# Packing two columns' bits into one f16 weight, and two last blocks of 68 rows

## The reference, cut to what is computed

```python
N, F, C = 5000, 128, 16                      # adj is 5000 x 5000 float32 of zeros and ones
# layer 0
w = adj * (y @ y.T)                          # y: one class of 16 for each row
w = w / maximum(w.abs().sum(1), 1e-12)
x = layernorm(x + 0.9 * (w @ x) + 0.1 * h0)
# layer 1, with adj for both of its matrices
f = tanh(adj * adj) * (adj > 0)              # tanh(1) where adj is one
new_adj = the 350 largest of each row of f   # a row has fewer than 350 ones
h2 = tanh(x @ W_proj + b_proj)
x = layernorm(x + relu(new_adj @ (h2 @ W_gcn) + b_gcn))
```

## Time and profile before

| | us |
|---|---|
| median of 3 runs | 467.92 (467.48 to 468.11) |
| the profiled execution | 467.66 |
| its span, first to last instruction | 465.9 |
| PE busy | 438.7 (94%) |
| DVE busy | 377.9 (81%) |
| ACT busy | 263.5 (57%) |
| POOL busy | 161.5 (35%) |
| adj's DMAs | about 3 to 259 |

### The profile page before, as it was taken

The page is one execution under the profiler, slowest core; times in us unless marked ns, Lnnn a source line. Parts: engine busy times, 40 slices in busy tenths (PEclk is TensorE's granted clock), DMA queues, the critical chain, the costliest instruction groups (busy, mean ns, idle before and its releaser), DMA issues.

```text
span 465.9 us, 15131 instructions
## 1 busy us (share of the span) xinstructions
PE 438.7 (94%) x5104; PEld 386.3 (83%) x5104; DVE 377.9 (81%) x1359; ACT 263.5 (57%) x355; POOL 161.5 (35%) x310
## 2 busy tenths in 40 slices
PE   3659999999999999999999999999999999999994
PEld 2448898888888988888888887888888888888883
DVE  5988999999999999999999976675575575575562
ACT  4997998999999999999999934900000000000000
POOL 3022543455444455554445541221211211211222
PEclk9977999999999999999999999999999999999998
DMA  8999999999999999999999200000000000000000
GB/s 262 411 414 420 419 417 417 415 408 411 409 422 420 422 423 420 424 423 412 417 419 422 60 2 1 13 11 17 17 11 17 17 11 17 17 11 17 17 11 23
DMA packets 25518, 108.50 MB, mean 233 GB/s; under 512 B 5097, under 2 KB 15490, under 8 KB 15490
## 3 DMA queue, kind: packets, MB, share of 16 engines
q1 hardware_dynamic: 25490, 108.14, 57.5%
HBM read 105.57 MB, written 2.56 MB: 232 GB/s over the span
## 4 chain that ended last, share of the span: by engine, by line
PE 75%; DVE 10%; ACT 5%; issue 5%; DMA 2%; POOL 2%; POOLq 0%; DVEq 0%; ACTq 0%; SPq 0%
PE acc L521 64%; PE words L471 6%; DVE a_bits L783 3%; DMA a_rows<-in_adj_dram 2%; PE feat_acc L584 2%; PE proj_acc L595 2%; ACT count_out L685 2%; DVE turned L870 2%; PE xnt_acc L576 1%; ACT count_out L678 1%; ACT x_parts L664 1%; POOL xs L438 1%; ACT count_out L754 1%; DVE z_high L921 1%; ACT count_out L746 1%
## 5 line engine op out<-in xcount | busy, mean ns | idle before, releaser
L521 PE MATMUL acc<-x_parts,turned 128*128 128x257 f16 (+1 forms) x1600 | 195.2, 276 | 3.2 <-DVE turned L870 1.0
L678 ACT ACTIVATE count_out<-a_rows,ones 128x2688 bf16<-128x2688 f32 (+1 forms) x80 | 190.2, 2377 | 0.5 <-DMA a_rows<-in_adj_dram 0.2
L521 PEld LDWEIGHTS acc<-x_parts,turned 128*128 128x128 fp8e4 (+1 forms) x1600 | 154.4, 98 | 28.9 <-issue 3.8
L521 PE MATMUL acc<-f_parts,turned 128*128 128x256 f16 (+1 forms) x1560 | 171.6, 273 | 0.8 <-DVE turned L870 0.8
L521 PEld LDWEIGHTS acc<-f_parts,turned 128*128 128x128 fp8e4 (+1 forms) x1560 | 152.0, 98 | 19.3 <-issue 1.3
L783 DVE TENSOR_SCALAR a_bits<-a_rows 128x2688 bf16<-128x2688 f32 (+1 forms) x80 | 116.7, 1459 | 2.7 <-DMA a_rows<-in_adj_dram 2.3
L421 POOL TENSOR_TENSOR var_eps<-mean_var,consts 128x1 f32<-128x1 f32 x80 | 18.6, 232 | 266.1 <-DVE mean_var L1077 139.7
L870 DVE TENSOR_SCALAR turned<-a_words 128x320 uint16 (+1 forms) x305 | 66.9, 233 | 53.2 <-PE acc L521 52.8
L424 POOL TENSOR_TENSOR rstd<-var_eps,consts 128x1 f32<-128x1 f32 x80 | 86.5, 1081 | 6.3
L870 DVE TENSOR_SCALAR turned<-same_class 128x320 uint16<-128x320 uint16 x313 | 71.3, 254 | 0.1
L471 PEld LDWEIGHTS words<-pack,a_bits 128*128 128x128 bf16 (+1 forms) x1600 | 51.3, 97 | 9.7 <-DVE a_bits L783 7.8
(11 more groups left out here) (111 smaller groups left out, 288.3 us busy)
## 6 DMA issues: line engine op xcount, KB each, us to landing
a_rows<-in_adj_dram SPq DMA_DIRECT2D x39, 1344.0 KB, 7.8
a_rows<-in_adj_dram SPq DMA_DIRECT2D x39, 1156.0 KB, 8.3
out_dram<-xn SPq DMA_DIRECT2D x39, 64.0 KB, 1.5
h_rows<-in_L_gnn_h_dram SPq DMA_DIRECT2D x19, 128.0 KB, 8.1
xs<-in_x_dram SPq DMA_DIRECT2D x3, 640.0 KB, 10.0
xs<-in_x_dram SPq DMA_DIRECT2D x1, 512.0 KB, 10.3
y_nat<-in_L_gnn_y_dram SPq DMA_DIRECT2D x1, 304.0 KB, 3.6
a_rows<-in_adj_dram SPq DMA_DIRECT2D x1, 84.0 KB
```

Source lines behind the costliest of these rows:

```text
L521: mm = pe.matmul(acc[par][0:m, 0:cols], bits, parts[:, b, 0:cols], start=first and b == blocks[0], stop=last and b == blocks[-1])
L678: act.activation(count_out[0:m, 0:w], a_rows[par][h][0:m, 0:w], ACT.Relu, bias=ones[0:m, 0:1], scale=-HUGE, accum_out=col).then_inc(s_coun ...
```

## The change

Rows and columns: there are now 38 full blocks, all in pairs, and the last 136 rows are two blocks of 68 (even and odd rows of them), so that still 40 blocks stand. Halves are 2560 and 2440 columns wide (20 column blocks each, 40 in all).

Packing: DVE writes a bit as a byte, 0x3C or 0x3D, into a uint8 tile. Two neighbouring bytes, which belong to the two blocks of a pair of columns, are read as one f16 weight. A packing matmul then takes 128 such weights (256 columns of adj), with `pack` as 128 x 17 f16; there are 10 a half, 20 a block. A word holds 8 rows of two columns; the count too is of two columns. ACT subtracts in `words_of` what the 0x3C bytes add up to, by a bias, with Relu and a scale; for the blocks of 68 rows in three pieces. Unpacking is eight shifts of 320 words a block as before (five for a block of 68 rows), but the fp8 bits of a column block now lie at every other byte, and the products read them so. In the setup, the packing weights need nine small steps on POOL in place of sixteen and three on DVE, the classes' words are made by half as many and as wide products, and the separate loads of block 0 of x, y and h0 are gone. SP loads h0 for a pair in odd steps, in place of even ones.

```diff
-BITS = 16
+BITS = 8
-    FULL = N // P
-    TAIL = N - FULL * P
-    NB = FULL + 1
+    FULL = N // (2 * P) * 2
+    TAIL = (N - FULL * P) // 2
+    NB = FULL + 2
+    COLS = NB // 2
     WORDS = P // BITS
-    HB = NB // 2 + 1
+    HB = NB // 2
+    HC = COLS // 2
...
     def rows_of(t):
-        return TAIL if isinstance(t, int) and t == LAST else P
+        return TAIL if isinstance(t, int) and FULL <= t <= LAST else P
...
     def rows_in(a, b, par, pair, cols):
-        if isinstance(b, int) and b == LAST:
-            return a[FULL * P:N, cols]
...
+        if isinstance(b, int) and b >= FULL:
+            return a[FULL * P:N, cols].rearrange("(p e) c -> e p c", e=2)[par]
+        v = a[0:FULL * P, cols].rearrange("(s p e) c -> e s p c", p=P, e=2)[par]
...
-        a_bits = [sb(f"a_bits{h}", [P, HB * P], BF16) for h in range(2)]
+        a_bits = [sb(f"a_bits{h}", [P, HB * P], U8) for h in range(2)]
...
-                for b in range(h * HB, HB if h == 0 else NB):
-                    c, d = column(b) - HALF[h].start, spacing(b)
+                for b in range(h * HC, h * HC + HC):
+                    c = (b - h * HC) * P
                     mm = pe.matmul(words[par][:, b * PITCH:b * PITCH + WORDS + 1],
-                                   a_bits[h][0:m, c:c + (P - 1) * d + 1:d], pack[0:m, :], start=True, stop=True)
+                                   a_bits[h][0:m, :].bitcast(F16)[:, c:c + P], pack[0:m, :], start=True, stop=True)
...
-                    bits = turned_at(n, par)[:, b, :].bitcast(F8)[:, 0:m]
+                    bits = turned_at(n, par)[:, b // 2, :].bitcast(F8)[:, b % 2:2 * m:2]
...
+                    if rows_of(n) == P:
+                        act.activation(to[:, :, 0:WORDS + 1], of[:, :, 0:WORDS + 1], ACT.Relu, bias=less_full, scale=UNIT)\
+                            .then_inc(s_words, 1)
+                        return
...
-                dve.tensor_scalar(a_bits[h][0:m, 0:w], a_rows[par][h][0:m, 0:w], 1.0, None,
-                                  ALU.is_equal).then_inc(s_bits, 1)
+                dve.tensor_scalar(a_bits[h][0:m, 0:w], a_rows[par][h][0:m, 0:w], 1.0, float(ZERO_BYTE),
+                                  ALU.is_equal, ALU.add).then_inc(s_bits, 1)
```

More of the change, by code:

```diff
@@ L77, in rows_in, with steps @@
     def rows_in(a, b, par, pair, cols):
-        if isinstance(b, int) and b == LAST:
-            return a[FULL * P:N, cols]
-        if isinstance(b, int) and b == 0:
-            return a[0:P, cols]
-        v = a[P:FULL * P, cols].rearrange("(s p e) c -> e s p c", p=P, e=2)[(par + 1) % 2]
-        if isinstance(b, int):
[L85 to L99, removed]
+        if isinstance(b, int) and b >= FULL:
+            return a[FULL * P:N, cols].rearrange("(p e) c -> e p c", e=2)[par]
+        v = a[0:FULL * P, cols].rearrange("(s p e) c -> e s p c", p=P, e=2)[par]
+        if isinstance(b, int):
+            return v[pair]
+        return v[bass.ds(pair, 1), :, :].rearrange("a p c -> p (a c)")
+    def steps(eng, step, lag, after={}, first=4):
+        first = max(first, lag + 2 + lag % 2)
         for t in range(first):
@@ L103, in steps @@
                 after[t]()
-        with eng.Fori((first - 1) // 2, (FULL - 1) // 2) as i:
+        with eng.Fori(first // 2, FULL // 2) as i:
+            step(i * 2, 0, i)
             step(i * 2 + 1, 1, i)
-            step(i * 2 + 2, 0, i + 1)
         for t in range(FULL, NB + lag):
@@ L121, in steps4 @@
             step(t, t % 2, t // 2, 0, t)
-        count = (FULL - first) // 4
-        with eng.Fori(0, count) as i:
+        with eng.Fori(0, (FULL - first) // 4) as i:
             for c in range(first, first + 4):
                 step(i * 4 + c, c % 2, i * 2 + c // 2, i, c)
-        for t in range(first + count * 4, NB + lag):
+        assert (FULL - first) % 4 == 0 and first % 2 == 0
+        for t in range(FULL, NB + lag):
             step(t, t % 2, t // 2, 0, t)
@@ L369, in step @@
                     load_rows(t, par, pair)
[L370 to L372 removed]
+                if valid(t - 1) and c >= 3 and par == 1:
+                    load_h0(t - 1, pair, i, c - 1)
+            steps4(sp, step, 4, 6)
             def store(t, par, pair):
@@ L388, in _ @@
                                base=0, pattern=[[-1, P]], channel_multiplier=1).then_inc(s_const, 1)
[L389 to L393, removed]
-                                       compare_op=ALU.not_equal, fill=float(1 << (bit + half * HALF_BITS)),
-                                       base=-(bit * 2 * WORDS + half), pattern=[[-2, WORDS]],
-                                       channel_multiplier=1).then_inc(s_pack, 1)
+            pool.wait_ge(s_pack, 2)
@@ L865, in unpack @@
                     dve.wait_ge(s_acc, n - 1)
-                last = HALF_BITS if m == P else 1
-                for bit in range(lo // 2, min(hi // 2, last)):
+                last = -(-m // WORDS)
+                for bit in range(lo, min(hi, last)):
                     shift = ONE_BIT - bit
```

253 lines of the change are left out of this document (134 added, 119 removed).

## The result

The changed kernel takes 489.65 us, median of its four runs, against 467.86 us for the kernel before on the same chip. One of the four took 2372 us; the other three have a median of 488.72 us (485.33 to 490.59), and by them the kernel takes 1.0436 times as long, with a 95% interval of 1.0365 to 1.0507. Forecast were 478.6 us (467 to 487) and slower: the direction is right, the time is past the upper end. The same kernel in a second set of runs took 485.41 us (483.08 to 486.02), 1.0364 times 467.83 (1.0332 to 1.0395). In all later runs of the kernel and of its variants nothing like it recurred; its cause is open, and so is whether the general path ran in it.

The account below looks back on a forecast made before the run. PE, DVE and the loads were taken as full at once, the loads' ceiling limiting gains; 467.66 + 8.0 (holding the steady -1.0) + 2.4 clock + 0.3 store = 478.4, with the runs' median 0.26 higher: 478.6 us, range 467 to 487.

Parts of the forecast that it names:

- An engine has moved 417.5 / 16 = 26.1 GB/s, four move 104, and 2.72 MB take 26.0 us: Last two blocks: four loads of 68 rows go to four engines; last packing +8.0 us, range 6.5 to 26.0 for the loads.
- The forecast's 15% on this rate: Last loads: uncertainty of the four engines' rate, 4 us to each side, used for the range 467 to 487.
- The steady part: Full blocks of layer 0: loads at their ceiling let PE's saving give only -1.0 us, 0 to 3 over 38 blocks.
- Cast, ten packings and hand-over: After the last half lands at 276.0: 1.35, 0.25 and 0.15 us, so the last packing ends at 277.8.
- The clock: After the last packing: PE's granted clock, lowered by the waits, slows products (+2.1) and packings (+0.3); +2.4 us, bounds 0 to 3.
- The end: Last store of 68 rows, 35 KB on four engines at 26.1 GB/s: +0.3 us.
- The number of engines: Loads of 68 rows: the most engines up to 16 that divide 68 are 4, DMA share near 0.25.
- the four waits in the last loads: Last loads: PE waits for DVE's cast, and that for a_rows, four times 3 to 5 us.
- casts at 1462 ns: DVE's cast to bytes: 0 added, near 1.46 us as before; bounds 0 to +1.45 us a half.
- the weights at every other byte: PE's products: byte-wise steps cost 0, loads near 97 ns; bounds 0 to tens of ns a product.
- packings at 24 ns: PE's packing matmuls: 24.3 ns each despite 17 columns, 20 a block, giving PE back 0.49 us a block.
- The rival of 16 engines: Last loads: all 16 engines serve 68 rows, 1.5 to 6 us gained, about 464; chance 0.12 for sixteen or eight engines.

Follow-up runs that it names:

- the split one: The changed kernel with each load of 68 rows in the two last blocks issued as one of 64 and one of 4 rows: 468.61 us, ratio 1.0003.

## Why the prediction was wrong in size and right in direction

**The step that failed: "An engine has moved 417.5 / 16 = 26.1 GB/s, four move 104, and 2.72 MB take 26.0 us".** Count, share and bytes were right, the rate wasn't. From 250 us on the trace moves 3.66 MB by 290.6, of which 2.72 are the last four loads; the other 0.94 need 2.2 us at 417.5, so the full loads end near 252.2 and the four take 38.4 us: 71 GB/s, 18 an engine. This term is +12.4 us. The second profiled execution, whose last packing ended 3.6 us earlier, comes to about 35 us and 77 GB/s in the same way. An engine's rate was taken from 16 engines with eight rows each. By themselves, loads of 68 rows moved 79 to 104 GB/s inside a group, but over a whole group of the kernel's four, until the last engine was done, 72 to 90. The kernel's 71 and 77 lie at the lower end of that. Alone, the four took 30 to 38 us where 26.0 were forecast, so about half of the excess or more belongs to loads of 68 rows themselves; what makes them slow and spread, and whether the rest of the kernel adds anything, is open. The forecast's 15% on this rate was too narrow: the one row with few engines at work (56 GB/s at a share of 0.47, 7.5 GB/s an engine) lay far below 26.1 and should have opened the range upward. And the clock's bounds gave 476 to 479 us, not the 475 to 481 of the forecast.

**The steady part, -1.0 us because the loads' ceiling sets it,** was wrong in size and cause. The full loads ended at 252.2, not 250.0: +2.2 us against the forecast. DVE sets the changed kernel's pace (6.31 us a step, busy for 137.1 of 140 us from 100 to 240; PE's packing twice and half the loads leave it, fewer unpackings shorten it), and the loads come next, at 6.21. I had read a share of 1.01 as the limit and DVE's 6.00 us between two casts of the earlier trace rows as a pace it could hold; the casts alternate between about 6.4 and 6.0, and only the mean over many is a pace: 6.249, not 6.22. The changed kernel's step is 0.06 us longer than before's with the same work on DVE. From 100 to 240 us DVE is idle for 2.88 us in place of 1.68, and the difference, about those 0.06 us a step, stands in front of the casts (1.6 us in place of 0.3). Half the loads and doubled packings leave 1.3 us of it, so neither the loads nor PE cause most of it; what does is open.

**Cast, ten packings and hand-over, 1.8 us:** 1.9 measured. 12.4 + 2.2 + 0.1 = 14.7, which is 292.5 - 277.8.

**The clock, +2.4 us because "after the last packing nothing covers it"**, was wrong. The granted clock did fall: 0.66 and 0.67 in the stretches, 20 products in 4.49 us at 286.01. But those 20 products come ahead of the last packing, and behind them the granted clock was back at 1.0 (0.82 from 290 to 291 in the mean): 0.41 us for the packings and 2.40 for the 20 products behind them, its full pace. The slow products lay in the wait for the last load. 0 instead of +2.4.

**The end:** +0.3 forecast for the store. Work from the last packing to the end became 1.65 us shorter. It isn't the wait that gave DVE and ACT time to catch up: the kernel with 8 loaded rows, whose last loads are short, has the same 196.2 us (its profiled execution's 466.81 - 270.63), and so has the split one. The traces place it: the long row of layer 1's products starts 18.9 us behind the last packing in before and 18.2 us in the changed kernel, so 0.7 us lie ahead of it and 0.95 in layer 1. What saves them wasn't tested.

Sum: 478.4 + 14.7 - 2.4 - 0.3 - 1.65 = 488.7.

**What was right.** The number of engines, by the share and again by 124 rows in the kernel before; the four waits in the last loads, though of 4.95, 6.68, 7.49 and 3.69 us on DVE and not of 3 to 5 each; casts at 1462 ns for 1460; the weights at every other byte (97 ns a load, the products' pace unchanged); packings at 24 ns though their moving side has 17 columns; PE's busy share down to 91%. Not foreseen: ACT's word copy takes 545 ns for 340 elements in place of 473 for 360, now with Relu and a bias; from 100 to 160 us no engine's idle time is put down to it. The rival of 16 engines ("about 464") would have failed as well: the kernel with 64-row loads is that case, and it took 468.6, because PE's saving is worth nothing, because a step became longer and not shorter, and, for about 1 us, because 16 engines into 64 partitions move 208 GB/s.

A version that keeps the two-byte weights and has the old last blocks (128 rows and 8) wasn't built; by an estimate from the kernel with 8 loaded rows it would not be far below 466.6. Nor was one built that lays 64 rows from partition 32 on, for which the computation of these blocks would have to move too. No version that computes everything beat the kernel before.

## What to carry to other kernels

Look at the row count of every load before its bytes: what decides is to how many DMA engines it can be dealt in equal shares and in which partitions it lands, and the last loads, which nothing hides, pay for it in full. A full DMA share doesn't prove that the loads are the limit: halve the bytes and see whether the step moves, and look at the first steps apart from the steady ones. When one of several nearly full engines gets less work, find the next one by its longest period, not by its shortest gap.

## What the runs showed of the hardware

- A load runs on as many engines, up to 16, as divide its rows evenly: 16 for 128 and 64 rows, four for 68, 76, 92 and 124, two for 34, one for 17 (by shares of about 1, 0.25, 0.13 and 0.06). 124 rows in place of 128 moved 88 GB/s and cost 23.6 us.
- 64 rows into partitions 0 to 63: 210 GB/s at a share of 1.02; into 32 to 95: 417. A full share says that engines are occupied, not that they move much.
- One, two or four DMA engines move 27 GB/s each with 17, 34, 76 or 92 rows. With 68 rows an engine moves 20 to 26 inside a group, 18 to 23 over a whole group of the kernel's four loads alone, and 18 and 19 in the kernel's two profiles. The cause is open.
- The cast from f32 to bytes runs as fast as to bf16 (0.58 ns an element), and weights read at every other byte load as fast as dense ones.
